# Soft-experts stage: the subtraction of the maxima on VectorE in pairs, and finishing and statistics of the sequences at other places in the plan

## What is computed

```python
x_ln = (x - mean) / jnp.sqrt(var + LN_EPS) * gamma + beta
x_n = _l2norm(x_ln, -1) * scale
mu_n = _l2norm(mu, 0)
logits = jnp.einsum('bnd,des->bnes', x_n, mu_n)          # 16 experts, 128 slots each
dispatch = jax.nn.softmax(logits, axis=1)                # over the rows
combine = jax.nn.softmax(logits.reshape(B, N, E * S), axis=-1)   # over all slots
slot_in = jnp.einsum('bnd,bnes->besd', x_ln, dispatch)
h = jax.nn.gelu(jnp.einsum('besd,edh->besh', slot_in, W1) + b1[None, :, None, :], approximate=False)
slot_out = jnp.einsum('besh,ehd->besd', h, W2) + b2[None, :, None, :]
out = jnp.einsum('bsd,bns->bnd', slot_out.reshape(B, E * S, D), combine)
...
x = _layernorm(x + out, axis=-1)
```

## Time and profile before

| | |
|---|---|
| median of 3 runs | 1222.25 us (1220.8 to 1222.49) |
| the profiled execution | 1219.74 us |
| its span in the trace | 1217.9 us |
| of it from 842.7 us on, the experts stage | 375 us |
| busy over the span | PE 94%, PEld 86%, DVE 67%, ACT 65%, POOL 58% |
| mean granted TensorE clock | 0.984 of full speed |

### The profile page before, as it was taken

How to read it: one execution, slowest core, us unless ns; L and a number is a source line. 1 busy time by engine, 2 the same in 40 slices (tenths; PEclk the granted TensorE clock), 3 DMA queues, 4 the chain that set the end, 5 groups by cost and what they waited for, 6 DMA issues and landing times. The chain is left out here.

```text
span 1217.9 us, 23566 instructions
## 1 busy us (share of the span) xinstructions
PE 1141.2 (94%) x8096; PEld 1048.8 (86%) x8096; DVE 811.7 (67%) x1899; ACT 790.7 (65%) x1654; POOL 710.9 (58%) x485
## 2 busy tenths in 40 slices
PE   4899999999989999999989999999899989888997
PEld 3798999898989998999989989998778879787986
...
DMA packets 48789, 47.57 MB, mean 39 GB/s; under 512 B 13080, under 2 KB 43288, under 8 KB 48416
## 3 DMA queue, kind: packets, MB, share of 16 engines
...
q10 hardware_dynamic: 288, 0.07, 0.0%
...
## 5 line engine op out<-in xcount | busy, mean ns | idle before, releaser
L536 PE MATMUL ring<-kT,qT 128*128 128x384 f32 (+5 forms) x1152 | 245.7, 349 | 9.8 <-ACT exps L701 3.9
L701 ACT ACTIVATE exps<-ring,neg_max 128x128 f32<-128x128 f32 (+7 forms) x256 | 189.2, 742 | 61.4 <-DVE neg_max L845 60.7
L845 DVE CUSTOM_DVE_ANT_0 ring<-ring,hidden 128x128 f32<-128x128 f32 (+7 forms) x256 | 191.4, 767 | 34.0 <-PE ring L536 33.3
L536 PEld LDWEIGHTS ring<-kT,qT 128*128 128x128 f32 x1152 | 186.3, 190 | 22.6 <-issue 5.4
L718 ACT ACTIVATE exp_parts<-turned 128x512 fp32r<-128x512 f32 x192 | 114.4, 596 | 134.9 <-PE turned L551 113.0
L551 PE MATMUL turned<-ident,exps 128*128 128x128 f32 x1152 | 178.7, 273 | 8.6 <-DVE exp_parts L863 4.5
L572 PE MATMUL mix<-exp_parts,v_parts 128*128 128x256 f32 x1152 | 183.8, 295 | 0.4 <-DVE exp_parts L863 0.4
L551 PEld LDWEIGHTS turned<-ident,exps 128*128 128x128 f32 x1152 | 141.6, 141 | 26.7 <-issue 7.4
L863 DVE TENSOR_TENSOR exp_parts<-turned,exp_parts 128x512 fp32r<-128x512 f32 x192 | 131.7, 686 | 33.2 <-ACT exp_parts L718 33.1
L973 POOL TENSOR_TENSOR cos_part<-taken,cos_sb 128x1024 f32<-128x1024 f32 x38 | 91.3, 2402 | 99.6 <-ACT taken L669 99.6
L572 PEld LDWEIGHTS mix<-exp_parts,v_parts 128*128 128x128 f32 x1152 | 148.8, 189 | 0.6 <-DVE exp_parts L863 0.6
...
## 6 DMA issues: line engine op xcount, KB each, us to landing
...
```

Source lines behind the costliest of these rows:

```text
L536: last = nc.tensor.matmul(ring_cols(item, half * BANK, piece), qT[:, H % QUERIES, a, i * P:(i + 1) * P], kT[:, G % 2, m, half * piece:(hal ...
L701: nc.scalar.activation(dst, tile, ACT.Exp, bias=neg_max[:, H % 2, i:i + 1], scale=-1.0, accum_out=row_sum[:, H % 2, i:i + 1]).then_inc(don ...
L845: nc.vector.tensor_tensor_reduce(tile, tile, later, -1.0, 3.0e38, ALU.add, ALU.min, neg_max[:, H % 2, i:i + 1]).then_inc(done[kind], 1)
```

## The change

`shift` moves from GpSimd to VectorE. Its four tiles of a unit are taken in two pairs: (0, 1) at the end of step `j == 3`, ahead of the next step's `run`, and (2, 3) at `j == 0` behind `top`, ahead of the `combine` of tiles 4 and 5. In the last unit all four (half tiles) stand behind `slot_last`. The statistics of sequence 1 move from steps 0 to 2 to ahead of the first `top`, and its last parts `inv_2` and `offsets` into the first step. `mixed`, the sum, gets one buffer for each sequence. `finish` and `stats_3` of sequence 0 move from steps 18 to 21 (1, 2, 3 and 2 tiles) to steps 18, 22 and 26 (3, 3 and 2 tiles), `vary_3` to step 26, `std_3` to 28, `inv_3` to 29, and all eight `normal_a` to the end of step 30 (before: four each at the ends of 26 and 27). `length` moves from step 11 to 12. The `turn_unit` items 2 and 3 of step 14 move ahead of `spread` 2 and 3. In units 2 and 6 the fourth `fold` of the unit ahead moves to the middle of the step two further on, ahead of the second `output`, and its copy `folded_b` behind `top`.

```diff
@@ -1003,3 +1003,3 @@
     def deviations(b):
-        put(*[(kind, b) for kind in ("vary", "std_1", "inv_1", "std_2", "inv_2", "offsets")])
+        put(*[(kind, b) for kind in ("vary", "std_1", "inv_1", "std_2")])
 
@@ -1044,3 +1044,10 @@
         put(("logits", g), *[("fold", u, i) for i in range(4)])
-        put(("top", g), (taker(0), u, 0), ("exp", g), (taker(1), u, 1), ("keep", g), (taker(2), u, 2))
+        if g == 0:
+            put((taker(0), u, 0))
+            if sequences > 1:
+                put(("inv_2", 1), ("offsets", 1))
+        put(("top", g))
+        if g:
+            put((taker(0), u, 0))
+        put(("exp", g), (taker(1), u, 1), ("keep", g), (taker(2), u, 2))
         put(("run", g), ("inverse", g), (taker(3), u, 3))
@@ -1060,4 +1067,2 @@
             return
-        if s == 2:
-            deviations(1)
         for j in {6: (0,), 7: (1, 2), 10: (3,)}.get(s, ()):
@@ -1066,4 +1071,2 @@
             put(("squares", 1, j))
-        if s == 11:
-            put(("length", 1))
         if s == 12:
@@ -1075,2 +1078,5 @@
     split_mu(2)
+    if sequences > 1:
+        moments(1, range(8))
+        deviations(1)
     begin(0)
@@ -1087,4 +1093,2 @@
         unfolded = live and u % 4 == 3
-        if s == experts + 6 and sequences > 1:
-            put(("vary_3", 0, 0))
         if changed:
@@ -1107,4 +1111,6 @@
             put(("gelu", v))
-        if s == experts + 8 and sequences > 1:
-            put(("std_3", 0, 0), ("inv_3", 0, 0))
+        if s == experts + 12 and sequences > 1:
+            put(("std_3", 0, 0))
+        if s == experts - 4 and sequences > 1:
+            put(("length", 1))
         if ahead and not change:
@@ -1112,3 +1118,3 @@
         if ripe and j == 1 and unfolded:
-            put(("output", v, 1))
+            put(("fold", u, 3), ("output", v, 1))
         if j in (1, 3) and live:
@@ -1117,3 +1123,6 @@
             put(("top", s + 1))
+        if ripe and j == 0 and not last_unit:
+            put(*[("shift", v, k) for k in (2, 3)])
         if ripe and j == 1 and unfolded:
+            put((taker(3), u, 3))
             slots(v, 1)
@@ -1121,4 +1130,2 @@
             split_mu(s + 3)
-        if s in (0, 1, 2) and sequences > 1:
-            moments(1, ((0, 1), (2, 3, 4), (5, 6, 7))[s])
         if s == experts - 2 and sequences > 1:
@@ -1151,3 +1158,2 @@
                     put(("keep", s + 1))
-                put(*[("shift", u, k) for k in range(4)])
         if j == 3 and live:
@@ -1156,3 +1162,4 @@
                 fold(u + 1, 2)
-                fold(u + 1, 3)
+                if u % 4 != 2:
+                    fold(u + 1, 3)
         if j == 3 and live and not ahead:
@@ -1174,2 +1180,4 @@
             spread(v - 1, (4, 5))
+        if j == 3 and ahead:
+            put(*[("shift", u, k) for k in range(2)])
         if ahead and not change:
@@ -1179,2 +1187,4 @@
             begin(s + 1)
+        if s == experts - 2 and sequences > 1:
+            turn_units(1, (2, 3))
         if j == 2:
@@ -1184,2 +1194,3 @@
             put(("slot_last", v, 0), ("slot_last", v, 1))
+            put(*[("shift", v, k) for k in range(4)])
             put(*[("weight", v, k, half) for half in range(2) for k in range(4)])
@@ -1191,4 +1202,2 @@
                     put(("output", v, 1))
-        if s == experts - 2 and sequences > 1:
-            turn_units(1, (2, 3))
         if s + 4 < total:
@@ -1201,5 +1210,9 @@
         if sequences > 1:
-            finish(0, {experts + 2: (0,), experts + 3: (1, 2), experts + 4: (3, 4, 5), experts + 5: (6, 7)}.get(s, ()))
-        if s in (experts + 10, experts + 11) and sequences > 1:
-            put(*[("normal_a", 0, 4 * (s - experts - 10) + t) for t in range(4)], ("store", 0, s - experts - 10))
+            finish(0, {experts + 2: (0, 1, 2), experts + 6: (3, 4, 5), experts + 10: (6, 7)}.get(s, ()))
+            if s == experts + 10:
+                put(("vary_3", 0, 0))
+            if s == experts + 13:
+                put(("inv_3", 0, 0))
+            if s == experts + 14:
+                put(*[("normal_a", 0, t) for t in range(8)], ("store", 0, 0), ("store", 0, 1))
     b = sequences - 1
@@ -1297,3 +1310,3 @@
         peak_wide = sb("peak_wide", [P, N])
-        mixed = sb("mixed2", [P, TILES, WIDE])
+        mixed = sb("mixed2", [P, B, TILES, WIDE])
         later = sb("later", [P, 2, 2, D])
@@ -1888,2 +1901,11 @@
                     nc.vector.tensor_tensor(kept(v, k)[:, 0:BANK], kept(v, k)[:, 0:BANK], peak_wide[:, 0:BANK], ALU.subtract).then_inc(done[kind], 1)
+                if kind == "shift":
+
+                    v, k = which
+                    dve.wait_ge(done["widened_a"], v + 1)
+                    dve.wait_ge(done["widened_b"], v + 1)
+                    dve.wait_ge(done["keep"], v * UNIT + k + 1)
+                    dve.wait_ge(done["run"], v * UNIT + k + 1)
+                    cols = slice(BANK if v == UNITS - 1 else 0, N)
+                    nc.vector.tensor_tensor(kept(v, k)[:, cols], kept(v, k)[:, cols], peak_wide[:, cols], ALU.subtract).then_inc(done[kind], 1)
                 if kind == "weight_lo_b":
@@ -1917,6 +1939,5 @@
                     dve.wait_ge(done["spread"], count("spread", v, t))
+                    b = v // PER
                     if v % PER == 0:
-                        if v:
-                            dve.wait_ge(done["vary_3"], count("vary_3", v // PER - 1, 0))
-                        nc.vector.tensor_copy(mixed[:, t, :], spread_ps[:, t % 2, 0:WIDE]).then_inc(done[kind], 1)
+                        nc.vector.tensor_copy(mixed[:, b, t, :], spread_ps[:, t % 2, 0:WIDE]).then_inc(done[kind], 1)
                     else:
...
@@ -1996,10 +2017,2 @@
                                             ).then_inc(done[kind], 1)
-                if kind == "shift":
-
-                    v, k = which
-                    pool.wait_ge(done["widened_a"], v + 1)
-                    pool.wait_ge(done["widened_b"], v + 1)
-                    pool.wait_ge(done["keep"], v * UNIT + k + 1)
-                    cols = slice(BANK if v == UNITS - 1 else 0, N)
-                    nc.gpsimd.tensor_tensor(kept(v, k)[:, cols], kept(v, k)[:, cols], peak_wide[:, cols], ALU.subtract).then_inc(done[kind], 1)
```

6 lines of the change are left out of this document (3 added, 3 removed).

## The result

The changed kernel takes **1235.62 us** (median of four executions, three of them at 1235.45 to 1235.74) against 1222.37 (1220.8 to 1226.26) for the kernel before on the same chip: ratio 1.0104, 95% interval 1.0083 to 1.0126. It is slower, by 13.3 us, where 18.3 were forecast from its profiled execution and 1240 us was said. The range of 1226 to 1246 contains it. The trace read here is that second one, since one execution of the first, the profiled one, took 2599.64 us with TensorE's matmuls at twice their usual time from start to end (814 ns for one of the attention layer's at L510, 398 in the second trace).

What follows compares the result with a forecast made beforehand. PE's work plus its waits bound the experts stage, with 0.2 us reserve ahead of tile 4's `combine`. Terms summed to 18.3 us slower, 1238.0 for the profiled execution and 1240.5 for the median, said as 1240; range 1226 to 1246.

Steps and rivals of the forecast that it cites:

- statistics first, and step 3: First folds wait 4.5 us for `folded_a`, plus 1.0 clock; step 3 loses its 1.66 wait: +3.8 us together.
- step 8: Second pair delays tile 4's `combine` (2.7 us), GpSimd collision adds 3.7, lower clock 1.6: +8.0 us.
- steps 12 and 28, with the gathers: Each place: `combine` wait 1.5, gather later by 1.4 behind `folded_b`, clock 1.5; +8.8 us for both.
- steps 14, 15 (`turn_unit`): With `turn_unit` ahead of `spread`, PE's waits of 0.93 and 1.06 go: -2.0 us.
- `finish` in threes: Finish tiles at steps 18, 22 and 26 delay VectorE by 1.9, 0.9 and 0.8: +3.6 us.
- step 20: A pair's wait of 2.7 + 1.5 clock replaces 5.24 + 1.9 behind `finish` tiles: -2.9 us.
- step 22, and 21: Wait for fourth weights at step 22, 3.63 + 1.5 clock, goes as `finish` and `vary_3` moved: -5.1 us.
- step 24: A pair's wait of 2.7 + 1.5 clock replaces 3.73 + 1.55, `std_3` and `inv_3` gone: -1.1 us.
- the end: `normal_a` ahead of `turned_a` +2.5, `inv_3` ahead of last weights +1.0, last `spread` waiting 1.0: +4.5 us.
- Short waits, cheap waits: Rival: no lower clock after waits near 3 us, no step 8 collision; 6.0 us slower, 1228; chance 0.27.
- Not reached: Rival: `combine` of tile 4 stays in time, five waits fall away; 1218 or 1221; 0.07 faster, 0.05 within 0.2%.
- Later still: Rival: finish tiles hide nothing (4.5 us more) and bring the low clock; 24 us slower, 1247; chance 0.09.

Runs made afterwards that it cites:

- e1: The changed kernel run once more with nothing edited, the source of the trace read: 1236.38 us, ratio 1.0117 to the kernel before.
- e5: The changed kernel with the second pair of subtractions moved behind the combine of tiles 4 and 5: 1222.77 us, ratio 1.0007 to the kernel before.
- e6: The changed kernel with the rows GpSimd scales at step 7 scaled one step later: 1232.48 us, ratio 1.0064 to the kernel before.
- e3: The changed kernel with the subtraction back on GpSimd, four in a row at its old places: 1217.59 us, ratio 0.9955 to the kernel before.
- e4: The changed kernel with the statistics of sequence 1 back at steps 0 to 2, `inv_2` and `offsets` with them: 1234.40 us, ratio 1.0073.
- e7: e3 with the fourth fold of units 2 and 6 back at its old place: 1214.06 us, ratio 0.9910 to the kernel before.
- e8: e7 with statistics at their old steps, `finish` in ones and twos, `vary_3` and `inv_3` later, `normal_a` split: 1205.26 us, ratio 0.9840 to the kernel before.
- e2: The kernel before with only the subtraction moved to VectorE, in pairs at the change's places: 1238.77 us, ratio 1.0136.
- e9: e8 with the subtraction on VectorE, none ahead of a combine that PE waits for: 1218.62 us, ratio 0.9969 to the kernel before.

## Why the prediction was right, and where it was off

The sign, the range and the mechanism hold. To compare term by term, I measured the stretch from each `logits` of PE to the next in both traces: the difference of the two lengths is what the change did there, waits and clock together. The 32 differences add up to the 14.4 us. (The profiled execution of e1 took 1237.83 us, and 1238.0 was said for it. That is luck: 3.7 us of it lie in the attention layer, and the stage's share is 14.4 for 18.3.)

| term | forecast | measured | from |
|---|---|---|---|
| statistics first, and step 3 | +3.8 | +3.8 | waits 1.52 and 2.37, clock 2.0; step 3 shorter by 2.1 |
| steps 4 to 7 | 0 | -1.1 | -0.6 at steps 4 and 5, a shorter stretch at the lower clock; -0.5 at step 6, fourth weights no longer late |
| step 8 | +8.0 | +7.9 | wait 5.81, 24 matmuls in 5.08 |
| steps 9 to 11 | 0 | -1.0 | fourth weights no longer late |
| steps 12 and 28, with the gathers | +8.8 | +10.2 | waits 1.67, 1.75 and twice 2.88 |
| steps 14, 15 (`turn_unit`) | -2.0 | -3.0 | waits of 0.34, 0.93, 1.06 gone |
| step 16 | +0.7 | +0.6 | wait of 0.43 |
| `finish` in threes | +3.6 | +4.0 | waits 1.89, 1.56, 0.90 ahead of the peaks |
| step 20 | -2.9 | -2.9 | 2.60 for 5.24, both slow behind |
| step 22, and 21 | -5.1 | -5.8 | no wait for weights |
| step 24 | -1.1 | -2.6 | 2.55 for 3.73, not slow behind |
| the end | +4.5 | +4.2 | waits 2.57 and 0.92, clock 1.7, less waits of 0.45 and 0.34 that are gone |
| sum | +18.3 | +14.4 | (rounded terms: 14.3) |

**What held.** The reserve of 0.2 us ahead of `combine` and a pair at 1.2 us an instruction gave 2.7 us for the waits at steps 20 and 24; 2.60 and 2.55 were there, and with the second pair moved behind (e5) they went. The collision at step 8 was put at 3.7 and is 3.3 (e6). The 1.5 at steps 12 and 28 is 1.67 and 1.75. The wait ahead of the gathers was put at 2.7 and is 2.88. The forecast's four large positive terms, start, step 8, the folds and the end, were each within 1.4 us. At the start two sizes were off and cancel: the waits of 4.5 are 3.9, and the clock behind them cost 2.0 and not 1.0. VectorE's part of it was near: the prediction's terms for `top` add up to 850.6, not the 850.8 that it gives, and `top` began at 854.17, which is 850.5 without the 3.7 us from the attention layer.

**The clock at step 24.** The prediction put 1.5 us on each wait above 2.5 and nothing on those below 2. The rows above speak against any such rule, and so does one place of the kernel before, at step 4, that it didn't read:

```profile
891.39 1.09 PE L1485 MATMUL ffn_turned<-ident,ffn_exps 128*128 128x128 f32 x8 [1.57 <-ACT ffn_exps L1680]
892.63 4.47 PE L1475 MATMUL ffn_ring<-xT,parts 128*128 128x512 f32 x12
```

The twelve matmuls take 3.0 us elsewhere, and the granted clock was 0.63 on average there. A wait of 2.55 us is followed by 24 matmuls in 3.17 us, one of 2.60 by 4.64, one of 1.67 by 3.16, one of 1.75 by 4.66; in e3 the same gather behind the same wait of 2.88 takes 3.57 in one place and 1.97 in the other. 3.05 us for 24 and 1.97 for the gather are the full clock. So between 1.6 and 2.9 us a wait was followed by the lower clock in some places and not in others, and I can't say from these traces why. It is not chance from run to run: in e4 and e6 too, 2.55 at step 24 and 1.67 at step 12 are followed by 3.13 to 3.15 us, 2.61 at step 20 and about 1.74 at step 28 by 4.49 to 4.67. As a sum it is near: besides step 8 and the start the forecast counted 1.5 at each of four places, 6.0; at six places the run had 1.59, 0.12, 0.11, 1.61, 1.45 and 1.57, which is 6.5, and 1.7 more at the end, where none was forecast. The single terms are off by up to 1.6 either way: too much at step 24, too little at step 28.

**What the weights gave back.** The prediction said that what GpSimd gives up is not on PE's path. Before, PE's second `spread` of step 10 was paced by the fourth tile of weights:

```profile
949.07 5.30 PE L1574 MATMUL ffn_spread<-ffn_slots,ffn_weights 128*128 128x258 f32 x39 [0.20 <-DVE ffn_weights L1892]
```

39 matmuls in 5.30 us, of which 4.96 is in proportion, behind a pause of 0.20, and more ahead of it: the stretch is 10.20 us long, and 9.38 in the changed kernel. No wait above 0.2 shows it. The same stretch takes 10.15 to 10.18 us in e3, e7 and e8, which subtract on GpSimd, 9.38 or 9.39 in e2, e4, e5 and e6, which subtract on VectorE in pairs, and 9.85 in e9. So with the subtractions on VectorE the fourth tile is there sooner. This is 0.8 us of gain that I put at nothing; it was missed because I read only the large waits in brackets. Step 6 shows the same: 9.84 us before, 9.37 with the change, 9.86 in e3. At `turn_unit` it was the same: a wait of 0.34 us and small gaps, another 1.0 us on top of the two waits that were counted.

**The end.** The sum is right by luck, two of its terms are not. ScalarE's eight `normal_a` stand ahead of `turned_a` as forecast, 4.03 us of them, and cost 2.57 (put at 2.5):

```profile
1194.49 4.03 ACT L1642 ACTIVATE y_sb<-y_sb,ffn_offset,ffn_inv 128x256 f32<-128x256 f32 x8
1198.43 0.57 ACT L1627 ACTIVATE ffn_dispatch<-ffn_turned 128x512 f32<-128x512 f32 x1
```

Behind that wait PE had the lower clock again, which the forecast didn't count there:

```profile
1199.39 1.86 PE L1556 MATMUL ffn_turned<-ident,ffn_run 128*128 128x128 f32 x8
1201.18 2.87 PE L1537 MATMUL ffn_small<-ffn_dispatch,ffn_folded 128*64 128x128 f32 x32
```

The kernel before took 1.11 and 1.97 for them: 1.7 us.

The last `spread` waits 0.92 us where 1.0 was forecast, but for ScalarE's exponentials of the half tiles, not for the `combine`. They wait for the half subtractions: e2 has the same 0.93 without any `normal_a` moved, and in e3 it is gone. The 1.0 for `inv_3` was not there: the change has no wait for the last weights. The waits of 0.45 for them and of 0.34 for `turned_a` that the kernel before had are gone, so the missing 1.0 and these 0.8 about cancel the 1.7 of the clock. In e3, with the subtraction on GpSimd and `inv_3` at the same place, the wait for the last weights is 1.63 us, where the kernel before had 0.45; so the term takes both, and the weights of the change came early enough to hide it.

**The rivals.** *Short waits, cheap waits* at 1228 needed the full clock behind all of these waits and no collision; four of six waits had the lower clock, and the collision was 3.3 us. *Not reached* is refuted by five waits. *Later still* (1247) wanted 4.5 us more from `finish`; it was 0.4 more. And the whole is not the sum of two halves: the subtraction alone costs 16.3 us, the rest alone saves 4.9, which gives 11.4; together they cost 13.9. At steps 20 and 24 the kernel before waited 5.24 and 3.73 us for `finish` and the factors, and e2 waits no longer, 4.72 and 3.42: the pair hides behind them. With them moved away (e3 against the change) it pays 2.60 and 2.55. Steps 12 and 28 go the other way, 2.62 and 2.60 in e2 and 1.67 and 1.75 in the change.
